# Causal attention scores from two-piece float32r stacks, two heads in the two 64-row halves of TensorE

## What is computed

```
q, k, v = x @ Wq, x @ Wk, x @ Wv          # layer 1: folded latent weights, and a rotation of half of each head
dot  = q . k * scale, masked to key <= query
out  = softmax(dot) @ v  @ Wo             # (2, 16, 2048, 2048) scores, never stored whole
x    = layernorm(x + out)
```

## Time and profile before

| | |
|---|---|
| median of three runs | 4685.25 us |
| the profiled execution, first to last instruction | 4682.8 us |
| TensorE, VectorE, ScalarE, GpSimd busy | 85%, 64%, 44%, 14% of the span |
| mean granted TensorE clock | 0.912 of 2.4 GHz |

### The profile page before, as it was taken

One profiled execution on the slowest core, in us unless ns is written; L12 is line 12 of the kernel. 1 busy time (PEld: TensorE's weight loads), 2 busy tenths in 40 slices (PEclk: granted clock), 3 DMA queues, 4 the chain that ended last, 5 costly groups with the idle time before them and its releaser, 6 DMA issues. The chain is left out here.

```text
span 4682.8 us, 61940 instructions
## 1 busy us (share of the span) xinstructions
PE 3969.1 (85%) x21496; PEld 1944.2 (42%) x21588; DVE 2984.5 (64%) x5645; ACT 2043.9 (44%) x3649; POOL 670.4 (14%) x526
## 2 busy tenths in 40 slices
PE   7889967989969967996959899589899698779967
PEld 5233344333345534553533333433334355445534
DVE  3878765978557722773259786768785676237723
ACT  2356632456635511553124566215566454125521
POOL 2000004000023201331130000130000222022211
PEclk8799988899989988998978999789999899889989
DMA  3211002111010011001031110030110100110010
GB/s 81 32 28 28 2 2 48 27 29 28 2 46 8 4 36 45 8 7 29 9 73 28 29 28 2 20 50 8 28 28 2 46 8 6 35 45 7 5 33 23
DMA packets 149777, 117.43 MB, mean 25 GB/s; under 512 B 41192, under 2 KB 141008, under 8 KB 148944
## 3 DMA queue, kind: packets, MB, share of 16 engines
q1 hardware_dynamic: 142544, 107.20, 11.2%
q10 hardware_dynamic: 6912, 6.11, 0.4%
HBM read 41.15 MB, written 4.19 MB: 10 GB/s over the span
## 5 line engine op out<-in xcount | busy, mean ns | idle before, releaser
L735 DVE TENSOR_REDUCE chunk_max<-banks 128x1 f32<-128x512 f32 (+3 forms) x2240 | 1403.8, 670 | 217.5 <-PE banks L627 133.7
L702 ACT ACTIVATE probs<-banks 128x1024 f32<-128x1024 f32 (+3 forms) x1280 | 1085.3, 896 | 863.8 <-PE banks L671 435.3
L624 PE MATMUL banks<-stack_k,stack_q 96*128 96x512 bf16 (+3 forms) x2560 | 844.3, 376 | 137.3 <-DMA stack_k<-parts 55.0
L667 PE MATMUL banks<-stack_q,stack_k 99*128 99x512 bf16 (+3 forms) x2560 | 701.4, 351 | 7.4 <-ACT probs L702 7.4
L643 PE MATMUL banks<-probs,values_group 128*17 128x512 f32 (+3 forms) x5120 | 593.6, 536 | 0.0
L624 PEld LDWEIGHTS banks<-stack_k,stack_q 96*128 96x128 bf16 x2560 | 248.0, 100 | 788.2 <-DVE chunk_max L735 503.5
L1224 ACT ACTIVATE probs_l<-banks,nmax 128x256 f32<-128x256 f32 x512 | 238.5, 471 | 488.1 <-DVE nmax L1343 488.1
L1496 PE MATMUL banks<-hnT,w 128*128 128x512 f32 x768 | 353.8, 622 | 20.3 <-DVE hidden L1560 16.9
L1095 PE MATMUL banks<-wqkv,hT 128*128 128x512 f32 x768 | 361.9, 609 | 7.2 <-DMA wqkv<-in_L_ffn_wqkv 7.2
L1274 POOL TENSOR_TENSOR inv_norm<-ssum,mhalf 128x8 f32<-128x8 f32 x128 | 211.0, 1648 | 819.2 <-DVE ssum L1314 812.9
L667 PEld LDWEIGHTS banks<-stack_q,stack_k 99*128 99x128 bf16 x2560 | 241.1, 99 | 204.0 <-ACT probs L702 58.5
(11 more groups left out here) (182 smaller groups left out, 4824.4 us busy)
## 6 DMA issues: line engine op xcount, KB each, us to landing
stack_q<-parts SPq DMA_DIRECT2D x384, 64.0 KB, 2.4
stack_k<-parts SPq DMA_DIRECT2D x384, 64.0 KB, 2.4
xpos<-in_c_xpos SPq DMA_DIRECT2D x4, 1792.0 KB
wqkv<-in_L_ffn_wqkv SPq DMA_DIRECT2D x12, 512.0 KB, 9.4
w<-in_L_ffn_w ACTq DMA_DIRECT2D x16, 341.0 KB, 5.8
x_tok<-in_L_attn_x SPq DMA_DIRECT2D x8, 512.0 KB
rope<-in_c_rope SPq DMA_DIRECT2D x2, 2048.0 KB, 7.8
hs<-x_tok SPq DMA_DIRECT2D x64, 64.0 KB
```

What stands on the lines that cost most here:

```text
L624: ins = pe.matmul(out, sq[0:KS, c, j0 + j, i * P:(i + 1) * P], sk[0:KS, cc, j0 + j, 0:width], start=True, stop=not diag, skip_group_check= ...
L667: ins = pe.matmul(ps[:, SCORE + j, off:CH], keys, sq[0:KS + PARTS, c, j, off:CH], start=True, stop=not diag, skip_group_check=True)
L702: act.activation(probs[:, s % 2, 2 * half:2 * half + 2, off:CH], ps[:, SCORE + 2 * half:SCORE + 2 * half + 2, off:CH], ACT.Exp)\
L735: dve.tensor_reduce(chunk_max[:, n % 2, j:j + heads, i, cc], bank[:, 0:heads * width].rearrange("p (h n) -> p h n", h=heads), AX.X, ALU.ma ...
```

## The change

The pieces become two, in float32r (`PARTS = 2`, `Q_PART = [0, 0, 1]`, `K_PART = [0, 1, 0]`), so a head's stack has 48 rows of 4-byte values, and 50 with the rows of maxima. Two heads of a group lie at rows 0 and 64, and their matmuls are issued one behind the other into two banks. The diagonal masks are split in the same halves: four matmuls of 64 rows instead of two of 128. A first-pass slot is a pair of heads in two banks, and VectorE reduces both at once. There are now three score banks and two double banks for slots. Each head has an exponential of its own. The order of TensorE comes from `interleave`, which lets estimated times decide. The probabilities lie in the space of the first group's pieces, and PV reads the values without a copy. In `project` two pieces are taken straight from the PSUM bank in layer 0.

```diff
-PARTS = 3
-Q_PART = [0, 0, 1, 0, 1, 2]
-K_PART = [0, 1, 0, 2, 1, 0]
+PARTS = 2
+Q_PART = [0, 0, 1]
+K_PART = [0, 1, 0]
+NPAIR = GH // 2
+HALF = P // 2
-def first_pass_slots():
...
+def item_slots(n):
+    g, c = ITEMS[n]
+    slots = []
+    for i in range(TPC):
+        if i < 2:
+            slots.append((n, (0, NPAIR, i, c)))
+        for p in range(NPAIR):
+            if i >= 2:
+                slots.append((n, (p, 1, i, c)))
+            slots += [(n, (p, 1, i, cc)) for cc in range(c)]
+    return slots
+def interleave():
...
+    while todo or s2 < 2 * len(STEPS) or pv < len(STEPS) or outputs:
+        options = []
...
+        start, _, what = min(options)      # of: outputs, first (slot), scores (a pair), pv
...
+                pe = start + 0.06 + w / 2400 + (0.25 if slot[1][3] == ITEMS[slot[0]][1] else 0.0)
...
# prepare: half masks
+                for i in range(3):
+                    for h in range(2):
+                        for at in (0, HALF):
+                            sp.dma_start(half_f[at:at + HALF, i, h, :], a["c_masks"][i, h * HALF:(h + 1) * HALF, :])\
+                                .then_inc(S["halves"], 16)
                 for i, n in enumerate(("q", "k", "v")):
                     sp.dma_start(wd[:, i, :, :], ...
+                dve.wait_ge(S["halves"], 16 * 12)
+                dve.tensor_copy(k["half"][:, :, :, :], half_f[:, :, :, :]).then_inc(S["masks"], 1)
# project, SyncE
-                for part in ("high", "mid", "low"):
-                    sp.wait_ge(S[part], NCH)
+                sp.wait_ge(S["ones"], 2)
+                ones_rows(sp, ones, stacks[1], S["ones_rows"])
+                sp.wait_ge(S["high"], NCH)
...
# project, ScalarE: high piece (layer 0 from the bank)
-                        act.copy(parts[...0...], vbuf[:, u % 2, :]).then_inc(S["high"], 1)
-                    if what == "split":
-                        act.copy(parts[...1...], rbuf[:, m % 2, :]).then_inc(S["mid"], 1)
+                            act.activation(part_of(u, 0), ps[:, n % 8, :], ACT.Copy, scale=qscale[:, 0:1])\
+                                .then_inc(S["high"], 1)
# project, VectorE, layer 0
-                            dve.tensor_scalar(vbuf[:, u % 2, :], ps[:, n % 8, :], qscale[:, 0:1], None, ALU.mult)
-                        dve.tensor_tensor(rbuf[...], vbuf[...], parts[...0...], ALU.subtract).then_inc(S["rest"], 1)
+                        dve.scalar_tensor_tensor(out=part_of(u, 1), in0=ps[:, n % 8, :], scalar=qscale[:, 0:1],
+                                                 in1=part_of(u, 0), op0=ALU.mult, op1=ALU.subtract)
# project, GpSimd, layer 1 (the add of L538 stays)
-                        pool.tensor_tensor(parts[...2...], rbuf[...], parts[...1...], ALU.subtract).then_inc(S["low"], 1)
+                        pool.tensor_tensor(part_of(u, 1), vbuf[:, u % 2, :], part_of(u, 0), ALU.subtract)
# attend, TensorE
+                    bank = FIRST_PASS + 2 * (m % NFP)
+                    for p in range(pairs):
+                        for at in range(2):
+                            rows = slice(at * HALF, at * HALF + KS)
+                            ins = pe.matmul(ps[:, bank + at, p * width:(p + 1) * width],
+                                            sq[rows, c, p0 + p, i * P:(i + 1) * P], sk[rows, cc, p0 + p, 0:width],
+                                            start=True, stop=not diag, skip_group_check=True)
+                    if diag:
+                        for h in range(2):
+                            for at in range(2):
+                                rows = slice(at * HALF, (at + 1) * HALF)
...
+                                ins = pe.matmul(out[:, :, width - P:width], half[rows, 0, h, :],
+                                                half[rows, 1, h:h + 1, :].to_broadcast([HALF, pairs, P]), ...)
+                def scores(s, h):
...
+                    q = GH * s + 2 * h
+                    if q >= 2:
+                        pe.wait_ge(S["exped"], q - 1)
+                    for at in range(2):
+                        rows = slice(at * HALF, at * HALF + KS + PARTS)
+                        ins = pe.matmul(ps[:, (q + at) % NSC, off:CH], sk[rows, kt // TPC, h, ...], sq[rows, c, h, off:CH], ...)
...
+                for what, i in ORDER:
...
# attend, ScalarE: one head each
+                        act.activation(probs[:, s % 2, j, off:CH], ps[:, (GH * s + j) % NSC, off:CH], ACT.Exp)
# attend, VectorE
-                dve.tensor_copy(vcur[:, g % 2, :, :, :], values[:, :, g * GH:(g + 1) * GH, :])
+                    dve.tensor_copy(b[:, 0, :], rows).then_inc(S["max_high"], 1)
+                    dve.tensor_tensor(b[:, 1, :], rows, b[:, 0, :], ALU.subtract).then_inc(S["bank_read"], 1)
...
+                    dve.tensor_reduce(chunk_max[:, n % 2, :, p0:p0 + pairs, i, cc],
+                                      ps[:, bank:bank + 2, 0:pairs * width].rearrange("p a (h n) -> p a h n", h=pairs),
+                                      AX.X, ALU.max).then_inc(S["bank_read"], 1)
```

More of the change, by code:

```diff
@@ L110 @@
+SLOTS, ORDER = interleave()
+SLOT_OF = {(n, what): m for m, (n, what) in enumerate(SLOTS) if what in ("maxima", "outputs")}
 LAST_SLOT = {n: m for m, (n, what) in enumerate(SLOTS) if len(what) == 4}
-def steps_slots(s):
-    return list(range(SLOTS_TO[s + 1], SLOTS_TO[s + 2]))
 class Stage:
@@ L351, in causal_attention, with parts @@
         o = xT_o[:, :].rearrange("p (n c) -> p n c", c=C)
[L352 removed]
+        probs = first[:, :].rearrange("p (b h n) -> p b h n", b=2, h=GH)
+        stacks = sb("stack_q0", [P, NCH, NPAIR, CH], F32R), sb("stack_k0", [P, NCH, NPAIR, CH], F32R)
+        def parts(rows, g, part, cols):
+            if g == 0:
+                return first[rows, part * T + cols.start:part * T + cols.stop]
+            return later[rows, g - 1, part, cols]
         project(k, b, layer, xT, parts, values, stacks)
         wo = sb("wo", [P, KT, C])
[L355 removed]
+        attend(k, parts, values, o, stacks, probs, wo, k["a"]["L0_attn_Wo" if layer == 0 else "L1_attn_Wc"])
         project_out(k, wo, o)
@@ L547, in project, with ones_rows @@
-    S.end()
-def attend(k, parts, values, o, stacks, wo, wo_in):
+                    if rot and what == "split":
+                        pool.wait_ge(S["high"], u + 1)
+                        pool.tensor_tensor(part_of(u, 1), vbuf[:, u % 2, :], part_of(u, 0), ALU.subtract)\
+                            .then_inc(S["low"], 1)
+    S.end()
+def ones_rows(eng, ones, stack_k, done):
+    for at in (0, HALF):
+        eng.dma_start(stack_k[at + KS:at + KS + PARTS, :, :, :].rearrange("p n h m -> p (n h) m").bitcast(F32),
+                      ones[:, :].rearrange("p (o m) -> p o m", o=1).to_broadcast([PARTS, NPAIR * NCH, CH])).then_inc(done, 16)
@@ L621, in first_pass @@
                     width = (i + 1) * P if diag else CH
-                    for j in range(heads):
-                        out = bank[:, j * width:(j + 1) * width]
-                        ins = pe.matmul(out, sq[0:KS, c, j0 + j, i * P:(i + 1) * P], sk[0:KS, cc, j0 + j, 0:width],
-                                        start=True, stop=not diag, skip_group_check=True)
-                        if diag:
-                            ins = pe.matmul(out[:, width - P:width], identb[:, :], k["mask_qk"][:, :], start=False,
-                                            stop=True, skip_group_check=True)
```

395 lines of the change are left out of this document (193 added, 202 removed).

## The result

The changed kernel takes **5021.2 us** (median of four runs, 5005.2 to 5029.6) against 4685.2 for the one before (4684.5 to 4687.4): a ratio of 1.072, 95% interval 1.070 to 1.073. It is slower, by 336 us, where 4330 was forecast. The profiled execution spans 5003.6 us at a mean granted clock of 0.868, before 0.912.

The account below looks back on a forecast made before the run. It took TensorE's column time to bound attend, VectorE 8% behind; four attends at 83 us saved, plus 26 in project, less 5 in prepare, make 353 us, so 4683 becomes 4330; range 4190 to 4640.

Parts of the forecast that it names:

- The price of a pair: TensorE in attend: two 512-column float32r matmuls in row halves run together, taken at 0.22 us.
- VectorE 338: VectorE's work in one attend falls from 390 us to about 338, through double reductions and dropped copies of values.
- ScalarE 306: ScalarE's work in one attend rises from 279 us to 306, with twice as many exponential instructions.
- project -8 and -5: Project: 8 us saved in layer 0 and 5 in layer 1, twice each, 26 us in all.
- The two rivals on the price of a pair, 0.43 or 0.86 us: Attend's pairs cost more: at 0.43 us, time 4690 to 4790, chance 0.12; at 0.86 or more, about 5650, chance 0.07.
- If TensorE stays the bound with its idle time as it is, 495 - 80 = 415: Attend: 80 us less TensorE work with unchanged idle time brings one execution from 495 to 415 us.
- tighter coupling: Attend: three score banks make pairs wait for exponentials; set against the gain from exponentials starting early, at no net cost.
- rival 1: Attend: the loop of three score and two slot banks decides; step 2.7 us, time 4450 to 4600, chance 0.13.
- Rival 2: Attend: granted clock falls from 0.93 to 0.8, attend 463 us, time about 4535, chance 0.08.
- hidden: Project: stack loads, with half as many issues, stay covered in layer 0 and 1, costing no time.
- inside the 0.98 of PV: Attend: changing the array's mode around PV adds nothing beyond the 0.98 us PV already takes.
- The alternative that it named and did not take: Attend: every change to and from row halves costs a further 0.13 us, 42 us per attend, time near 4500.

Follow-up runs that it names:

- e9b: Changed kernel with two edits: no slot ordered before its stack is loaded, and idle matmuls before first pairs after the last maxima; 4754.6 us, ratio 1.016.
- e12: e10b with TensorE's order taken from estimated times, SP's queue included, instead of the order of the kernel before; 4578.6 us, ratio 0.977.
- e1: Changed kernel with the fixed order by column counts of the kernel before in place of the order by estimated times; 4924 us, ratio 1.051.
- e13: e12 with three score banks, an exponential per head, four single slot banks and the order remade from the same estimates; 5109.0 us, ratio 1.090.
- e15: e12, same order, with an exponential for each head instead of one for two; 4589.6 us, ratio 0.980.
- e3: Changed kernel with two idle matmuls before each step's first score pair once the last maxima are done; 4878.5 us, ratio 1.042.
- e2: Changed kernel whose order by estimates also models SP's queue, so no slot is ordered before its stack is there; 4849.7 us, ratio 1.036.
- e4: Changed kernel with both heads of a pair reading the lower half's rows, so matmuls share array rows; 6716.9 us (one run).
- e10b: Changed kernel with one-bank, one-head slots, four score banks, exponentials of two heads and the order of the kernel before; 4597.6 us, ratio 0.982.
- e11: e10b with an idle 128-row matmul in front of each slot before the first score of an attend; 4829.5 us, ratio 1.031.

## Why the prediction was wrong

**Right.** The price of a pair (0.22 taken, 0.24 found) with one record each; VectorE 338 against 339; ScalarE 306 against 314; the first exponential 10 to 20 us into attend (14); project -8 and -5 (-7.4, -4.4, -7.7, -4.8). The two rivals on the price of a pair, 0.43 or 0.86 us, did not occur. Prepare was +8 where 5 was taken: the twelve issues cost 7.60 us, 0.63 each, more than the 0.45 of the earlier trace rows.

**The step that failed** is "If TensorE stays the bound with its idle time as it is, 495 - 80 = 415", and the sentence after it that set the early start against "tighter coupling" at no net cost. TensorE's idle time did not stay: 32 us in one attend before, 111 after. Nor did its busy time fall by 80: 463 before, 465 after, and 437 in e9b without its idle matmuls (458 less 21), at before's clock. The first part of attend is not where the time went: the last reduction ends 408 us into it in e12 and 421 in the changed kernel. The second pass had fallen behind by then, and was left alone for 155 us instead of 66. Three terms stand behind it.

1. *The loop of three score banks.* The text named it, as rival 1, and sized it at 1.0 us for a pair (an exponential 0.5, a hop 0.1, a pair with its drain 0.4), PV adding 0.2 to a step: 2.2. Measured, the loop of a pair is 0.54 from the pair to its exponential and 0.65 from that to the next pair, 1.19, where the forecast had 0.4 and 0.6, and the step is 2.66. In e1 these two and PV's 0.99 and 0.43 are the whole of a step of 2.61; in the changed kernel PV stands behind the next step's first pair only, and so waits for the exponentials of its own step's last pair too, which the forecast left out. That the changed kernel cannot make these waits up with slots, since TensorE takes its queue in order, is argued and not measured by itself. A fourth bank takes attend from 609 to 478 and the step from 2.66 to about 2.0 (e13, e15), with slots of one head in both.
2. *The clock.* Rival 2 had it fall to 0.8 if TensorE worked 2.1 of 2.5 us, chance 0.08, as a case of its own. It is no case of its own: it follows from the waits. A TensorE that waits for exponentials in each step was given 1.2 GHz for part of the time, and there the step is 4.05 us, so that it falls further behind; the 27 us in front of a stack are followed by 1.2 GHz too (0.50 in the window from 1185). Filling the last stretch alone gives back 31 us per attend (e3). Of the 0.84 granted, the other part lies where nothing was filled. Rivals 1 and 2 came together, 2.66 at 0.84, and were weighed as alternatives; 4535 and 4600 were both too low for that.
3. *The stacks.* No rival held that TensorE would wait for a stack. `interleave` lets slots run as far ahead as VectorE can take them, but from the third group on a stack may be loaded only after the last outputs of the group two before it are read, since it takes that group's place, and then takes 24 issues of 0.67 us with four DMAs of rows of maxima among them, and the landing: for the last group 28 us from the first issue to TensorE's start (1182.4 to 1210.2). The prediction said "hidden" for project's stack and did not ask it for the other two; once the first pass ran ahead, the cover was gone. 38 us per attend (e2).

What remains of 87 us after 2 and 3 are mended (e9b, 520) is 25 us above before, and the fourth score bank with slots of one head takes 42 more than that off (e15, 478).

**Why even the good versions give 20 us per attend and not 80.** In e12 TensorE is busy 460 of 474 us at a clock of 0.94, against 463 at 0.93 before, so its own work fell by little. Two reasons can be read from the traces. With slots of one head, 336 of the 640 first-pass matmuls of an attend of e12 start without another score matmul within 15 ns, so half of them run without a partner, at 0.22 us where half a pair costs 0.12: 336 x 0.1, an estimate, is 34 us.

The other is the change between row halves and PV's column strips. The Trainium skill (TensorEngine Tiling (Array Packing), Key Properties) says that a change of tiling mode drains TensorE; the trace of e15 agrees, in so far as at the full clock a pair followed by a pair takes 0.24 us, one followed by a PV that waits for nothing 0.42 (1214.31 to 1214.73), and the first one behind PV 0.34 (1215.72 to 1216.06). (0.18 + 0.10) x 160 steps, an estimate, is 45 us of an attend, of which before paid a part too: 0.52 from two slots to PV where two cost 0.44, 13 us. The prediction had held this cost to be inside the 0.98 of PV; it stands in front of PV and behind it. The alternative that it named and did not take, 0.13 us more twice a step and 42 us per attend, was the nearer one.

**Left open.** No kernel had four score banks and double banks for slots: that takes nine. With three score banks double slots (e2, 544) did better than single ones (e13, 609), but the orders and the clock (0.85 and 0.79) differ as well, so what the double reductions are worth by themselves was not measured. Why the start of attend stays at the lower clock (below) is open too.

## What to carry to other kernels

Before an edit takes a bank from a ring, write down the ring's loop from starts in the timeline, hops included (here 0.54 and 0.65 around a 0.5 us exponential), and put into it whatever shares the in-order queue; if that is near the step, count on it, and count the lower clock on top as its consequence. Totals of work per engine can all be right and say nothing of the time. An order that runs one stream ahead needs its loads in its model.

## What the runs showed of the hardware

- Two matmuls of 48 to 50 rows in float32r, in the two row halves and into two banks, cost 0.24 us together for 512 columns at the full clock, one record each (after, 1059.95 to 1060.19).
- Dense records alone don't make the upper clock. With all score and mask matmuls in one half, one after the other, the granted clock was 0.51 for a whole attend with records over 93% of it (e4); matmuls in one half at a time do not explain that by themselves, since about half of e12's first-pass matmuls run so at a mean of 0.94; at the start of attend it was 0.50 for 75 us at 98% (e10b) and for 133 us at 98% (e11), there with a matmul of 128 rows in front of each slot. In e10b and e11 it rose only after the second pass and PV had begun. The Trainium skill (TensorE: Matmul & The Clock Gate, What's actually happening) says that activity releases the throttle; e3 agrees (0.76 to 0.98 by filling waits), e11 does not by its records, and what counts as activity these runs do not show.
